# Query projections moved from a phase of their own into the per-head attention loop

## The reference, cut to what matters

```python
qkv = jnp.einsum('bsd,ed->bse', x, w_qkv) + b_qkv        # x: 4 x 2048 x 2048
q, k, v = ...                                            # 16 heads of 128
scores = jnp.einsum('bhqd,bhkd->bhqk', q, k) / math.sqrt(Hd)
attn = softmax(scores + causal)
out = jnp.einsum('bsd,ed->bse', attn @ v, w_out) + b_out
x = _layernorm(x + out)
x = _layernorm(x + ffn(x))                               # silu(g) * u, gate/up 8192 wide
```

## Time and profile before

| | |
|---|---|
| two runs | 3428.54 and 3687.49 us, median 3558.02 |
| the profiled execution, own time | 3436.17 us |
| its span, slowest core (4) | 3434.6 us |
| spans of the eight cores | 3417.8 to 3434.6 us |
| mean granted TensorE clock by core | 0.870 to 0.877 of 2.4 GHz |
| busy: PE, ACT, DVE, POOL | 74%, 31%, 26%, 2% |

### The profile page before, as it was taken

One profiled execution on the slowest core, in us unless ns is written; L12 is line 12 of the kernel. 1 busy time (PEld: TensorE's weight loads), 2 busy tenths in 40 slices (PEclk: granted clock), 3 DMA queues, 4 the chain that ended last, 5 costly groups with the idle time before them and its releaser, 6 DMA issues.

```text
span 3434.6 us, 35393 instructions; the slowest of 8 cores (3417.8 to 3434.6 us)
## 1 busy us (share of the span) xinstructions
PE 2534.3 (74%) x12009; PEld 1157.3 (34%) x12224; DVE 908.0 (26%) x1908; ACT 1079.6 (31%) x1678; POOL 63.0 (2%) x117
## 2 busy tenths in 40 slices
PE   2986666667666666639329999988865999988882
PEld 0433333333333333224104444433322444433330
DVE  0023333333333333322332222211113222221112
ACT  0133333333333333320244333322232333332222
POOL 1000000000000000000000000000001000000001
PEclk9998888887888887759659999989987999999996
DMA  7510000000011100124122222212114222221113
GB/s 126 86 25 13 13 13 13 13 13 13 13 17 17 18 11 3 44 80 74 6 31 74 80 75 76 79 49 62 50 26 112 76 75 79 74 68 56 55 49 55
DMA packets 46125, 164.04 MB, mean 48 GB/s; under 512 B 5888, under 2 KB 6016, under 8 KB 45952
## 3 DMA queue, kind: packets, MB, share of 16 engines
q1 hardware_dynamic: 29808, 103.04, 11.4%
q0 software_dynamic: 16144, 58.73, 8.9%
HBM read 193.21 MB, written 8.39 MB: 59 GB/s over the span
## 4 chain that ended last, share of the span: by engine, by line
PE 59%; ACT 13%; DVE 12%; issue 10%; DMA 3%; DVEq 3%; ACTq 1%; POOL 0%; POOLq 0%; SPq 0%
PE OPp L753 14%; PE SB L678 13%; PE SB L675 12%; ACT AWa L382 6%; ACT AWa L398 4%; PE OPp L431 4%; PE SB L207 3%; PE SB L569 3%; PE SB L277 3%; DVE AWa L420 2%; PE PTa L408 2%; DVE wbf L736 2%; DVE AWa L363 2%; PE SB L355 2%; DVEq L371 2%
## 5 line engine op out<-in xcount | busy, mean ns | idle before, releaser
L678 PE MATMUL SB<-AWa,wbf 128*128 128x512 bf16 x2048 | 779.1, 380 | 110.3 <-ACT wbf L648 53.2
L675 PE MATMUL SB<-AWa,wbf 128*128 128x512 bf16 x1966 | 748.5, 381 | 0.0
L753 PE MATMUL OPp<-AXa,wbf 128*128 128x512 bf16 x2006 | 495.6, 409 | 111.0 <-DVE wbf L736 98.2
L277 PE MATMUL SB<-AXa,wbf 128*128 128x512 bf16 x1985 | 544.7, 432 | 9.3 <-issue 2.6
L382 ACT ACTIVATE AWa<-AWa,negm 128x512 f32<-128x512 f32 (+1 forms) x320 | 213.9, 669 | 747.2 <-DVEq L377 747.2
L753 PEld LDWEIGHTS OPp<-AXa,wbf 128*128 128x128 bf16 x2048 | 210.3, 104 | 396.4 <-issue 191.4
L277 PEld LDWEIGHTS SB<-AXa,wbf 128*128 128x128 bf16 x2048 | 217.3, 109 | 313.9 <-issue 152.3
L675 PEld LDWEIGHTS SB<-AWa,wbf 128*128 128x128 bf16 x2048 | 200.6, 98 | 350.8 <-issue 110.1
L678 PEld LDWEIGHTS SB<-AWa,wbf 128*128 128x128 bf16 x2048 | 200.8, 98 | 242.6 <-issue 2.8
L694 DVE SCALAR_TENSOR_TENSOR AXa<-SB,usc_s,gsb 128x512 bf16<-128x512 f32 x128 | 96.1, 751 | 655.6 <-ACT gsb L689 655.6
L730 ACT ACTIVATE wbf<-stg,c 128x2048 bf16<-128x2048 uint8 x64 | 127.9, 2001 | 436.7 <-PE OPp L753 376.6
(11 more groups left out here) (76 smaller groups left out, 1480.4 us busy)
## 6 DMA issues: line engine op xcount, KB each, us to landing
stg<-wgu SPq DMA_DIRECT2D x128, 512.0 KB, 3.5
stg<-wd SPq DMA_DIRECT2D x64, 512.0 KB, 3.7
wbf<-wqkv POOLq DMA_DIRECT2D x48, 512.0 KB, 5.2
AXa<-xkv POOLq DMA_DIRECT2D x16, 512.0 KB, 29.8
AXa<-xq POOLq DMA_DIRECT2D x1, 8192.0 KB, 28.9
wbf<-wout POOLq DMA_DIRECT2D x16, 512.0 KB, 5.1
yt<-AZa POOLq DMA_DIRECT2D x32, 256.0 KB, 3.9
mbc<-m_row SPq DMA_DIRECT2D x4, 256.0 KB, 11.2
```

The source lines that it names most:

```text
L277: e.matmul(SB[:, b * 512:(b + 1) * 512], wbf[wb_i][:, dc * 128:(dc + 1) * 128], Xbkv[:, dc * 2048 + tc * 512: dc * 2048 + tc * 512 + 512], ...
L675: e.matmul(SB[:, gb:gb + 512], wbf[sg_][:, dc * 128:(dc + 1) * 128], rr, start=(dc == 0), stop=(dc == NDC - 1)))
L678: e.matmul(SB[:, ub:ub + 512], wbf[su_][:, dc * 128:(dc + 1) * 128], rr, start=(dc == 0), stop=(dc == NDC - 1)))
L753: e.matmul(OPp[:, ob: ob + 512], wbf[q % 4][:, (ic % 16) * 128:(ic % 16) * 128 + 128], Hbuf[:, ic * 512:(ic + 1) * 512], start=(ic == 0), ...
```

## The change

The query phase is gone. The query projection of one head becomes two more units of the same kind (unit 8 for tokens 0 to 511, unit 9 for tokens 512 to 1023), so a head has ten units. Head 0 runs all ten up front. In the head loop the tile j = 6 runs units 6 and 9 of the next head, and the tile j = 7 units 7 and 8 (`proj_unit_mm(h + 1, 15 - j)`). The load of the query weights goes to the head of `kv_dma`, which now issues three loads, query, key, value, into buffers `(3 * hh) % 4`, `(3 * hh + 1) % 4` and `(3 * hh + 2) % 4` of the same four. The score matmuls of a tile wait for the unit that made their half of the queries.

```diff
-        for fc in range(NH):
-            need("gpsimd", f"wbf{fc % 4}")
...
-            ev_tok[fc] = eS.n
-        q_evac_done = eS.n
+        q_evac_done = 0
...
         def kv_dma(hh):
-            kb, vb = (2 * hh) % 4, (2 * hh + 1) % 4
+            qb, kb, vb = (3 * hh) % 4, (3 * hh + 1) % 4, (3 * hh + 2) % 4
+            need("gpsimd", f"wbf{qb}")
+            W("gpsimd", dG, dG.n)
+            I("gpsimd", dG, lambda e, hh=hh, qb=qb: e.dma_start(
+                wbf[qb][:], wqkv_d.ap()[hh].rearrange("p c f -> p (c f)")), 16)
+            qd = dG.n
+            I("gpsimd", eG, lambda e: e.drain())
+            qt_ = eG.n
             need("gpsimd", f"wbf{kb}")
...
+            kind = "v" if unit < 4 else ("k" if unit < 8 else "q")
...
+                if kind == "q":
+                    rhs = Xbkv[:, dc * 2048:(dc + 1) * 2048].rearrange(
+                        "p (a b2 f) -> p a b2 f", a=8, b2=2)[:, tc * 4:(tc + 1) * 4, 0:1, :]
...
+            if unit >= 8:
+                used(f"wbf{qb}", eT)
...
+                I("scalar", eS, lambda e, hh=hh, b=b, tc=tc: e.activation(
+                    QT[:, hh * 1024 + tc * 512: hh * 1024 + tc * 512 + 512],
+                    SB[:, b * 512:(b + 1) * 512],
+                    AF.Identity, bias=bqs[:, hh:hh + 1], scale=QK_SCALE))
+                qt_done[hh][tc] = eS.n
...
-        for u in range(8):
+        for u in range(10):
...
-                    if h == 0 and j == 0 and kc < 2:
-                        W("tensor", eS, q_evac_done)
+                    if kc == 0:
+                        W("tensor", eS, qt_done[h][j // 4])
...
                     u_mm = proj_unit_mm(h + 1, j)
+                    u_mm2 = proj_unit_mm(h + 1, 15 - j) if j >= 6 else None
...
                     proj_unit_evac(h + 1, j, *u_mm)
+                    if u_mm2 is not None:
+                        proj_unit_evac(h + 1, 15 - j, *u_mm2)
```

More of the change, by code:

```diff
@@ L239, in build_nc @@
         kvinfo = {}
+        qt_done = {}
         kt_ready = {}
@@ L258, in kv_dma @@
             vt_ = eG.n
-            kvinfo[hh] = (kb, vb, kd, kt_, vd, vt_)
+            kvinfo[hh] = (qb, kb, vb, qd, qt_, kd, kt_, vd, vt_)
             kt_ready[hh] = [None] * 4
+            qt_done[hh] = [None, None]
         def proj_unit_mm(hh, unit):
-            kb, vb, kd, kt_, vd, vt_ = kvinfo[hh]
+            qb, kb, vb, qd, qt_, kd, kt_, vd, vt_ = kvinfo[hh]
             b = 2 + (unit % 2)
[L265 to L273, removed]
+            kind = "v" if unit < 4 else ("k" if unit < 8 else "q")
+            tc = unit if unit < 4 else (unit - 4 if unit < 8 else unit - 8)
+            wb_i = {"v": vb, "k": kb, "q": qb}[kind]
+            dtok, gtok = {"v": (vd, vt_), "k": (kd, kt_), "q": (qd, qt_)}[kind]
+            W("tensor", dG, dtok)
+            W("tensor", eG, gtok)
             W("tensor", eS, unit_evac[unit % 2])
             for dc in range(NDC):
-                f = (lambda e, wb_i=wb_i, dc=dc, b=b, tc=tc:
+                if kind == "q":
+                    rhs = Xbkv[:, dc * 2048:(dc + 1) * 2048].rearrange(
+                        "p (a b2 f) -> p a b2 f", a=8, b2=2)[:, tc * 4:(tc + 1) * 4, 0:1, :]
+                else:
+                    rhs = Xbkv[:, dc * 2048 + tc * 512: dc * 2048 + tc * 512 + 512]
+                f = (lambda e, wb_i=wb_i, dc=dc, b=b, rhs=rhs:
                      e.matmul(SB[:, b * 512:(b + 1) * 512],
                               wbf[wb_i][:, dc * 128:(dc + 1) * 128],
-                              Xbkv[:, dc * 2048 + tc * 512: dc * 2048 + tc * 512 + 512],
-                              start=(dc == 0), stop=(dc == NDC - 1)))
+                              rhs, start=(dc == 0), stop=(dc == NDC - 1)))
                 if dc == NDC - 1:
@@ L289, in proj_unit_mm, with proj_unit_evac @@
                 used(f"wbf{kb}", eT)
-            return eT.n, b, is_v, tc
-        def proj_unit_evac(hh, unit, mm_tok, b, is_v, tc):
+            if unit >= 8:
+                used(f"wbf{qb}", eT)
+            return eT.n, b, kind, tc
+        def proj_unit_evac(hh, unit, mm_tok, b, kind, tc):
             W("scalar", eT, mm_tok)
-            if is_v:
+            if kind == "v":
                 need("scalar", f"stg{tc // 2}")
@@ L300, in proj_unit_evac @@
                 vt_ready[hh] = eS.n
-            else:
+            elif kind == "k":
                 need("scalar", f"kt{hh % 2}")
@@ L333, in build_nc @@
         kv_dma(0)
-        for u in range(8):
-            mtok, b, isv, tc = proj_unit_mm(0, u)
-            proj_unit_evac(0, u, mtok, b, isv, tc)
+        for u in range(10):
+            mtok, b, kind, tc = proj_unit_mm(0, u)
+            proj_unit_evac(0, u, mtok, b, kind, tc)
         for h in range(NH):
```

## The result

The changed kernel takes 1.0047 times the time of the kernel before, 95% interval 1.0034 to 1.0059: slower by some 16 us, and within 2% no change; I had forecast 34 us on the same side. Its median is 3448.22 us; the profiled execution took 3453.27 us (span 3451.7 on core 0; the other cores 3431 to 3449).

A forecast was written before the change was run, and what follows sets the result against it. PE bounds the query phase; in the head loop nothing is full, each tile being a round trip. Start -80 us, 14 heads at +8.1 each +113, head 14's tile 6 +1.5: net +34, 3470 us, range 3430 to 3518.

The forecast's parts named there:

- The start: Program start without the query phase: PE starts at 78.4 us, head 0's ten units end at 115.7; gain 80 us.
- T0: First transposes of tile 0 of head 0: forecast at 134.1 us instead of 214.23.
- (d): From unit 8's end to the next head's unit 0: key load, then value load, then drain; 12.7 us.
- (e): Unit 0 itself, on the low clock after the idle gap: 5.6 us, bounds 3.4 and 6.8.
- (b): Tile 6: what its two units take beyond the room there, 1.6 us a head.
- (a): From the transposes of tile 0 to the first unit of tile 7: 63.7 us.
- (c): Two units in tile 7 at full clock: 7.2 us, up to 2.5 more if the clock is low at first.
- (f): From the end of unit 0 to the transposes of tile 0: 0.1 us.
- The hidden wait: Rival at unit 0: value load there in time, a head costs only 1.6 us more; 3367 us, chance 0.05.
- The cheaper wait: Rival at unit 0: quickest loads (11.4 us), unit of 4.2, +5.4 us a head; 3431 us, chance 0.15.
- The low clock for the extra units: Rival in tiles 6 and 7: each extra unit up to 2.2 us longer, +12.6 a head; 3538 us, chance 0.15.

The follow-up runs named there:

- wait alone: Kernel before, with its key and value loads of the next head also waiting for the last unit of this head's tile 7; ratio 1.0185.
- more work in 6: Kernel before with 16 matmuls of 128x512, results unused, added ahead of tile 6's own unit; ratio 1.0074.
- values first: Changed kernel with its three loads per head issued as value, key, query; 3333.57 us, ratio 0.973 to the kernel before.
- chain of three: Changed kernel with its key load issued twice in a row, so three loads stand between unit 8 and unit 0; ratio 1.0328.

## Why the prediction was right or wrong, point by point

**The mechanism was right, a size was off.** A wait for two loads in a row at each head's first unit gives back all of the start's gain: shown by undoing it (0.973), by taking one load out of it (0.9731), by making it alone (1.0185) and by adding a load (1.0328).

**The start.** Forecast: first matmul 78.4, last unit 115.7, T0 134.1. Measured on core 0: 79.29, 116.74, 134.18; over eight cores T0 is 132.4. Right.

**(d) The chain.** 12.7 forecast, 12.28 measured, inside the bounds and far from the 9.4 that the prediction set beside it. PE idles 7.25 us of it in the mean of eight cores (on core 0 7.1: 175.5 less 79.3 at the start and 11.15 in head 0, over 12 more waits), not some 5: the work in between takes less time than I had left for it, and that saves nothing. **(e) The first unit.** 5.6 forecast, 5.86 measured; its clock is 0.50 at 307 us, and filling the wait brings it to 4.56. The Trainium skill (TensorE: Matmul & The Clock Gate, section "HAM oscillation — how this bites in real kernels") says that a loop that waits for loads between bursts starts each burst on the low clock; the trace agrees: the mean is 5.86 against 3.91, and each of the 112 first units that it is taken over needed more than 3.8 us.

**(b), the step that failed.** I took tile 6's extra as "the ends of 15 values with mean 1.6", from the clock that each old unit had met, and left (a) at 63.7: 65.3 for both. Measured 63.4, 1.9 less, where the kernel before has 63.5. These are the mean durations of the tile's own work and what PE then idles, heads 1 to 14, eight cores:

| | tile 5: unit, gap | tile 6: unit(s), gap | tile 7: unit(s), gap |
|---|---|---|---|
| before | 4.07, 2.63 | 5.16, 2.09 | 4.85, 3.07 |
| changed | 4.60, 2.10 | 7.81, 0 | 7.87, 0.2 |
| wait alone | 4.45, 2.25 | 4.44, 2.76 | 5.09, 2.84 |
| more work in 6 | 3.77, 2.91 | 8.76, 0 | 4.07, 3.73 |
| values first | 3.77, 2.89 | 8.39, 0 | 7.82, 0.2 |
| chain of three | 3.94, 2.73 | 8.13, 0 | 7.95, 0.1 |

From tile 6's unit to tile 7's the changed kernel takes 13.70 us against 13.57: +0.13, not +1.6. Two things make the difference.

The first is the clock that the pair met. It ran at full speed in 53% of the heads, where the old unit did in 15%, so the transposes start 0.5 us later behind the unit's start (7.76 against 7.25) instead of 1.6. The stretches on the low clock had moved: into tile 5, whose gap swallows them. The wait alone moves them in the same way (4.45 and 4.44, with no extra unit; 44% at full speed). But it isn't simply that there is a wait: with the longer wait of three loads, in which PE idles 13.15 us instead of 7.25, tile 6 is the slow one again (18% at full speed), as it is with no wait (values first, 7%), and with the wait filled by matmuls it lies between (37%). Why a wait of one length in tile 0 moves the low stretches and a longer one does not is not settled.

The second is a credit that my sum lacked, and that the runs show: behind a filled gap the tile's own work is quicker. From tile 6's transposes to tile 7's unit it takes 5.94 us instead of 6.32, and 5.91 to 5.95 in the last three rows of the table too. With more work in tile 6 alone the transposes come 1.35 us late (8.60 against 7.25), but tile 7's unit only 0.9 later behind tile 6's (14.48 against 13.57). So even at the old places of the low clock 1.6 was too much.

The terms together: -1.9 here, +0.65 at (c), -0.4 at (d), +0.3 at (e), and -0.3 at (f), as the transposes now start right behind the unit. That makes 89.2 instead of 90.9; the head before is 82.46 over eight cores and not core 4's 82.8. So 8.1 a head were forecast and 6.75 measured, and 14 x 1.35 = 19 us is 34 less 15.

**(c) Two units in tile 7.** 7.2 forecast, 7.87 measured: 0.65 short, for the clock was low at the start of the pair in most heads (the pair took over 7.3 us in 87 of 112). I had argued that filling tile 6 would hold it up, with up to 2.5 more if not; it didn't hold it.

**Rivals.** The hidden wait (0.05) is out. The cheaper wait (0.15) missed by as much as my forecast, on the other side, and its terms weren't there: a chain of 11.4 and a unit of 4.2. The low clock for the extra units (0.15) came in part, 0.65 in tile 7, far from its 2.2 in each tile. That the change would stay inside 2% held.

## What to carry to other kernels

When work moves into a loop, look at what it does to the last reader of each buffer: put the load that is needed first on the buffer that comes free first. Here the order of three loads was worth 3.2% (1.0047 to 0.973), and moving the last reader one tile forward 2.7% (to 0.9776). A unit in an idle gap can be free and can even pay, since what stands behind it runs at the higher clock (tile 7 of the kernel before, -0.60 us a head); it can also cost (tile 6, +1.2). So terms read from rows at one clock hold only as long as the low stretches stay where they were.

## What the runs showed of the hardware that I had not expected

Sixteen unused matmuls of 128x512 in each head's tile 7 made the whole kernel 0.43% faster (0.9941 to 0.9973), and twenty in front of a wait took back the full 0.47% that the change had cost. And the stretches on the low clock are not tied to the gap that looks largest: a wait in tile 0 in which PE idled 3 us moved them, five tiles on, from tile 6 (unit 5.16 to 4.44 us) to tile 5 (4.07 to 4.45), and one in which it idled 13 us (the chain of three) left them in tile 6.
